# Self-attention softmax sums: four matrix products per key tile, or GpSimd additions and one product per head group

## The chip, the cores and the metric

The kernel is one program on one core of a Trainium2 chip. The metric is device microseconds (us) of that core for the whole program, the median of several executions. Five engines matter here: PE (TensorE, the matrix products), PEld (its weight loads), DVE (VectorE), ACT (ScalarE), POOL (GpSimd); SP (SyncE) issues most of the DMAs.

## The reference, cut to what matters

The program is a gated memory attention, then a decoder block: causal self-attention with 16 heads of 32, a cross-attention, and a feed-forward layer. The change is in the causal self-attention, for a batch of 4 and 512 tokens:

```python
scores = jnp.einsum('bhqd,bhkd->bhqk', q * scale, k)
scores = jnp.where(mask, scores, jnp.finfo(jnp.float32).min)   # causal
p = jax.nn.softmax(scores.astype(jnp.float32), axis=-1).astype(q.dtype)
ctx = jnp.einsum('bhqk,bhkd->bhqd', p, v)
```

The kernel keeps the exponentials unnormalised, computes `exp @ v` and the sums of the exponentials over the keys, and multiplies the rows by the inverse of the sums at the end. It is the way to these sums that the change touches.

## The kernel before

`self_attention()` handles 16 groups (`NG`) of four heads each. Keys are cut into `ST` = 4 tiles of 128; because of the causal mask, key tile `kt` needs only the queries from `kt * 128` on, so its width is 512, 384, 256 and 128 queries a head. Scores are laid out with keys on partitions and queries along the row.

A group has 11 steps (`NU`), one for each of its `score_units`: four of key tile 0 (one head each, 512 wide), four of tile 1 (384 wide), two of tile 2 (two heads of 256), one of tile 3 (four heads of 128). In step `v` PE issues, in an order written out by hand:

- `scores(v + 2)`: mask and score products (L1015, L1018) into one of three PSUM banks;
- one unit of side work for a later group, `fill` (L990, L993: scores with queries on partitions, from which DVE takes row maxima, L961; or L998, a "turn", which turns the maxima of a group so that DVE, L965, and two DMAs of SP can put them as an extra row beside the queries);
- `values(v - 1)`, which does something only behind the last unit of a key tile (steps 4, 8, 10 and step 0 of the next group): four products with the values (L1036) and four with a matrix of ones (L1040), the latter being the sums. The four products of a set write four bands of 32 PSUM partitions, one for each head;
- a second `fill` in one step of each group.

ACT turns each unit of scores into exponentials in the tile `pT_s` (L937), a ring of 3 key tiles. After three units of the next group it copies both PSUM banks, values and sums, to `osb_s` in one instruction (`keep_sums`, L928). DVE then takes the inverses of the sums in four pieces of 128 queries (the "flip" items, L952), one at the head of each of its steps 4 to 7, between the row maxima (L961) that PE's fills feed. DVE does its items strictly in the order of `self_side_work`. POOL waits for the four pieces, multiplies values by inverses (`scale_rows`, L911) and issues the DMA of the result (L914). SP loads queries, keys and values in rings of 4 groups. The side work runs 8 units ahead of its own group, so groups 14 and 15 have little or none of it. Behind the last group DVE alone takes one inverse of 512 (L969) and multiplies (L972).

## Time and profile before

| what | value |
|---|---|
| time, median of 3 runs | 2597.75 us (2596.82 to 2597.81) |
| the profiled execution: its own time | 2612.24 us |
| the profiled execution: span of the trace | 2610.4 us |
| mean granted TensorE clock | 0.886 |
| busy over the span | PE 82%, PEld 53%, DVE 61%, ACT 38%, POOL 18% |
| exponentials L937 | x176, 96.0 us |
| scaling on POOL L911 | x15, 19.1 us |

The span is what the trace covers, from the first to the last instruction; the run's own time is 1.8 us more. Busy time of PE is modelled from pipelined instructions, so a full PE row does not mean that it is at its peak. Start times in the trace are microseconds from the start of the span. Self-attention lies between about 817 and 1052 us.

### The profile page before, as it was taken

Reading aid. Unit: us, or ns where it says so; the run is one execution under the profiler, and the core shown is the slowest. Engines: PE = TensorE matmul, PEld = TensorE weight load, DVE = VectorE, ACT = ScalarE, POOL = GpSimd, SP = SyncE. Lnnn points to the kernel's source line nnn. Section 1 sums busy time; section 2 is a strip of 40 time slices with the busy share of each in tenths; the row PEclk is TensorE's granted clock in tenths of the full one; section 3 lists DMA queues with packets and bytes.
Section 4 is the critical chain, followed back from the end, with each engine's and each line's share of the span. In section 5 each row is a group of like instructions: output and inputs, shape, how many; then the busy total and the mean of one; then the engine's idle time right before and its main releaser. Section 6 shows DMA issues by size and latency. Waiting matters only on the chain. (4 is left out here: it accounts for less than half of the span.)

```text
span 2610.4 us, 33805 instructions
## 1 busy us (share of the span) xinstructions
PE 2129.8 (82%) x12621; PEld 1385.1 (53%) x12638; DVE 1594.5 (61%) x2296; ACT 979.1 (38%) x1723; POOL 469.2 (18%) x474
## 2 busy tenths in 40 slices
PE   5985985985985999447346389999999879999968
PEld 3663664664673555345235234444443457787856
DVE  5186186286284776525325589999998157657544
ACT  1132132132131555123123058888888522222101
POOL 0221221121120111201202002222222312222111
PEclk8987987987986999768777579999999989999979
DMA  4025025025037663474563924444442033333332
GB/s 149 29 78 202 29 81 199 29 87 194 25 95 188 160 163 79 138 158 88 182 157 96 171 39 85 83 80 82 86 87 59 16 115 89 108 105 97 90 95 70
DMA packets 219855, 271.57 MB, mean 104 GB/s; under 512 B 53886, under 2 KB 136450, under 8 KB 217882
## 3 DMA queue, kind: packets, MB, share of 16 engines
q1 hardware_dynamic: 211548, 258.12, 38.8%
q0 software_dynamic: 7856, 10.90, 1.6%
q8 instruction: 116, 1.90, 0.3%
q14 instruction: 47, 0.39, 0.0%
q10 hardware_dynamic: 288, 0.27, 0.0%
HBM read 202.64 MB, written 64.47 MB: 102 GB/s over the span
## 5 line engine op out<-in xcount | busy, mean ns | idle before, releaser
L1521 DVE TENSOR_REDUCE quarters<-ps 128x2 f32<-128x804 f32 x512 | 483.1, 992 | 51.7 <-PE ps L1555 50.0
L1486 ACT ACTIVATE pT_x<-ps 128x512 f32<-128x512 f32 (+1 forms) x832 | 451.5, 595 | 104.0 <-PE ps L1583 76.5
L190 DVE TENSOR_TENSOR w_lo<-w_raw,w_hi 128x512 fp32r<-128x512 f32 (+2 forms) x357 | 278.0, 779 | 12.2
L188 DVE CAST w_hi<-w_raw 128x512 fp32r<-128x512 f32 (+2 forms) x357 | 176.2, 494 | 171.0 <-PE ps L196 93.8
L1555 PE MATMUL ps<-kx_ring,qx_ring 63*128 63x402 f32 x1024 | 234.2, 470 | 47.2 <-DMA kx_ring<-cross_k_by_part 35.4
L1598 PE MATMUL ps<-pT_x,vx_ring 128*17 128x256 f32 (+1 forms) x3328 | 261.4, 387 | 0.2 <-ACT osb_x L1468 0.2
L1555 PEld LDWEIGHTS ps<-kx_ring,qx_ring 63*128 63x128 f32 x1024 | 100.3, 193 | 239.8 <-DVE quarters L1521 124.1
L194 PE MATMUL ps<-mi_h,w_hi 128*128 128x512 f32 (+1 forms) x440 | 175.3, 398 | 34.8 <-issue 24.1
L1583 PE MATMUL ps<-qx_ring,kx_ring 64*128 64x512 f32 (+1 forms) x832 | 175.0, 417 | 6.2 <-ACT pT_x L1486 2.6
L196 PE MATMUL ps<-mi_l,w_hi 128*128 128x512 f32 (+1 forms) x440 | 174.0, 396 | 0.0
L195 PE MATMUL ps<-mi_h,w_lo 128*128 128x512 f32 (+1 forms) x440 | 173.8, 395 | 0.0
L1739 POOL TENSOR_TENSOR sg<-sg,keep_all 128x512 f32<-128x512 f32 (+1 forms) x55 | 87.6, 1592 | 413.3 <-ACT sg L1718 413.3
L961 DVE TENSOR_REDUCE row_max_s<-ps 128x1 f32<-128x384 f32 (+3 forms) x176 | 109.4, 633 | 75.5 <-PE ps L993 74.7
L194 PE MATMUL ps<-att_h,w_hi 128*128 128x512 f32 (+1 forms) x128 | 46.3, 361 | 121.4 <-POOL att_l L1099 121.4
L937 ACT ACTIVATE pT_s<-ps 128x512 f32<-128x512 f32 (+1 forms) x176 | 96.0, 558 | 128.7 <-PE ps L1018 126.6
L1598 PEld LDWEIGHTS ps<-pT_x,vx_ring 128*17 128x17 f32 (+1 forms) x3328 | 55.6, 95 | 111.0 <-issue 70.6
L194 PEld LDWEIGHTS ps<-mi_h,w_hi 128*128 128x128 f32 (+1 forms) x440 | 83.0, 189 | 55.4 <-issue 36.3
L993 PE MATMUL ps<-k_ring,q_ring 96*128 96x128 f32 (+3 forms) x256 | 90.5, 414 | 24.9 <-DMA k_ring<-self_k_by_part 24.9
L1111 DVE TENSOR_TENSOR own<-att_in,keep_expert 128x512 f32<-128x512 f32 x32 | 52.2, 1632 | 93.5 <-DMA att_in<-self_rows_by_batch 93.5
L194 PE MATMUL ps<-xh,w_hi 128*128 128x512 f32 x96 | 44.3, 461 | 76.9 <-DVE xl L304 76.9
L1718 ACT ACTIVATE sg<-ps 128x512 f32<-128x512 f32 (+1 forms) x55 | 32.8, 596 | 191.4 <-PE ps L196 191.4
L332 DVE RECIPROCAL rq<-ps 128x4 f32<-128x4 f32 x4 | 0.7, 184 | 166.9 <-PE ps L415 166.9
(262 smaller groups left out, 4480.1 us busy)
## 6 DMA issues: line engine op xcount, KB each, us to landing
kx_ring<-cross_k_by_part SPq DMA_DIRECT2D x96, 200.2 KB, 7.4
w_raw<-L_xattn_l_qkv SPq DMA_DIRECT2D x48, 256.0 KB, 3.1
w_raw<-L_xattn_v_qkv SPq DMA_DIRECT2D x48, 256.0 KB, 2.7
q_ring<-self_q_by_part SPq DMA_DIRECT2D x48, 256.0 KB, 4.2
k_ring<-self_k_by_part SPq DMA_DIRECT2D x48, 256.0 KB, 6.7
w_raw<-L_xattn_l_gate SPq DMA_DIRECT2D x40, 256.0 KB, 2.9
w_raw<-L_xattn_l_up SPq DMA_DIRECT2D x40, 256.0 KB, 2.9
w_raw<-L_xattn_l_down SPq DMA_DIRECT2D x40, 256.0 KB, 2.7
```

The source lines that it names most:

```text
L188: nc.vector.tensor_copy(hi, raw).then_inc(s_high, 1)
L190: nc.vector.tensor_tensor(out=lo, in0=raw, in1=hi.bitcast(f32), op=ALU.subtract).then_inc(s_split, 1)
L194: nc.tensor.matmul(dst, ah, bh, start=start, stop=False, **how)
L195: nc.tensor.matmul(dst, al, bh, start=False, stop=False, **how)
L196: return nc.tensor.matmul(dst, ah, bl, start=False, stop=stop, **how)
L937: nc.scalar.activation(pT[:, u % 3, j:j + n, 0:width], heads_of(ps[:, SCORES + v % 3, :], n, width), ACT.Exp, scale=SCALE).then_inc(s["s_e ...
L961: nc.vector.tensor_reduce(out=row_max[:, g % 2, j:j + heads, q], in_=heads_of(bank, heads, (q + 1) * P), axis=AX.X, op=ALU.max)\
L1486: nc.scalar.activation(pT[0:kn, u % 3, j, :], ps[0:kn, 5 + v % 3, :], ACT.Exp, scale=SCALE)\
L1521: nc.vector.tensor_reduce(out=quarters[:, g % 2, pair, :, q, quarter], in_=ps[:, at:at + 2, 0:MAXW], axis=AX.X, op=ALU.max)\
L1555: last = nc.tensor.matmul(ps[:, at + par, 0:MAXW], q_r[rows, g % RING, pair, q * P:(q + 1) * P], k_r[rows, g % RING, pair, k0:k0 + MAXW], ...
L1583: nc.tensor.matmul(ps[0:kn, 5 + (v + par) % 3, :], k_r[rows, g % RING, pair, k0:k0 + kn], q_r[rows, g % RING, pair, :], start=True, stop=T ...
L1598: last = nc.tensor.matmul(ps[j * HD:j * HD + CHD + 1, 4, queries], v_r[0:kn, g % RING, kt, j, :], pT[0:kn, u % 3, j, queries], start=kt == ...
```

## The change

POOL adds up the exponentials of a group's four key tiles into a new tile `acc_s`, and PE multiplies that one by the matrix of ones, once for a group (`total`), in step 3 of the next group. The tile `pT_s` keeps only tiles 1 to 3; tile 0's exponentials are written by ACT straight into `acc_s` (`exponentials`), a ring of 3 groups. POOL's order in a group is now: add tile 1 (`add_up(g, 1)`), scale the rows of the group before, add tile 2, add tile 3. ACT's copy is split in two, the values after three units of the next group (`keep_rows`), the sums after six (`keep_sums`), with a semaphore each. The four flips move from DVE's steps 4 to 7 to steps 6 to 9.

```diff
--- before.py
+++ after.py
@@ -814,7 +814,7 @@
             start, feed, given, by_step = feed[:first], feed[first:], 0, []
             for v in range(groups * steps):
                 g, i = divmod(v, steps)
-                now = [("flip", g - 1, i - 4)] if g and 4 <= i < 8 else []
+                now = [("flip", g - 1, i - 6)] if g and 6 <= i < 10 else []
                 due = -(-(v + 1) * (maxima + 1) // steps)
                 while feed and given < due:
                     now.append(feed.pop(0))
@@ -826,7 +826,7 @@
         def self_attention():
 
             RING, KQ_LOADS = 4, 6
-            names = ("s_kq0 s_kq1 s_kq2 s_kq3 s_v0 s_v1 s_v2 s_v3 s_one s_fill s_used s_so s_sh s_sc s_exp s_pv s_ob "
+            names = ("s_kq0 s_kq1 s_kq2 s_kq3 s_v0 s_v1 s_v2 s_v3 s_one s_fill s_used s_so s_sh s_sc s_exp s_pv s_acc s_sum s_ob s_os "
                      "s_rq s_at s_up0 s_up1 s_last s_end")
             ctx, sems = stage(names)
             s = dict(zip(names.split(), sems))
@@ -847,9 +847,15 @@
                 v_r = sb("v_ring", [P, RING, ST, P], ctx=ctx)
                 row_max = sb("row_max_s", [P, 2, 4, ST], ctx=ctx)
                 shift = sb("shift_s", [4 * ST, 2, P], f32r, ctx=ctx)
-                pT = sb("pT_s", [P, 3, 4, S], ctx=ctx)
+                pT, acc = sb("pT_s", [P, 3, 4, S - P], ctx=ctx), sb("acc_s", [P, 3, 4, S], ctx=ctx)
                 osb, att = sb("osb_s", [P, 2, 2, S], ctx=ctx), sb("att_s", [P, 2, S], ctx=ctx)
                 rq_rows = sb("rq_rows_s", [P, S], ctx=ctx)
+
+                def exponentials(u, j, n, width):
+
+                    g, kt = divmod(u, ST)
+                    later = g * (ST - 1) + kt - 1
+                    return pT[:, later % 3, j:j + n, 0:width] if kt else acc[:, g % 3, j:j + n, 0:width]
 
                 def heads_of(bank, n, width):
 
@@ -913,31 +919,60 @@
                             pool.wait_ge(s["s_at"], g + 1)
                             pool.dma_start(att_d[g // GB, :, g % GB, :], att[:, g % 2, :]).then_inc(s[f"s_up{g % 2}"], 16)
 
-                        for g in range(NG - 1):
-                            scale_rows(g)
+                        def add_up(g, kt):
+
+                            v = max(i for i in ends if ends[i] == kt)
+                            pool.wait_ge(s["s_exp"], NU * g + v + 1)
+                            if kt == 1:
+                                pool.wait_ge(s["s_pv"], ST * g + 1)
+                            else:
+                                pool.wait_ge(s["s_acc"], (ST - 1) * g + kt - 1)
+                            rest = acc[:, g % 3, :, kt * P:S]
+                            nc.gpsimd.tensor_tensor(out=rest, in0=rest, in1=exponentials(ST * g + kt, 0, 4, S - kt * P), op=ALU.add)\
+                                .then_inc(s["s_acc"], 1)
+
+                        for g in range(NG):
+                            add_up(g, 1)
+                            if g:
+                                scale_rows(g - 1)
+                            add_up(g, 2)
+                            add_up(g, 3)
                         for i in range(2):
                             pool.wait_ge(s[f"s_up{i}"], 16 * (NG // 2 - i))
 
                     @block.scalar
                     def _(act):
-                        def keep_sums(g):
+                        def keep_rows(g):
 
                             act.wait_ge(s["s_pv"], ST * (g + 1))
                             if g >= 2:
                                 act.wait_ge(s["s_at"], g - 1)
-                            nc.scalar.activation(osb[:, g % 2, :, :], ps[:, VALUES:SUMS + 1, :], ACT.Copy).then_inc(s["s_ob"], 1)
+                            nc.scalar.activation(osb[:, g % 2, 0, :], ps[:, VALUES, :], ACT.Copy).then_inc(s["s_ob"], 1)
+
+                        def keep_sums(g):
+
+                            act.wait_ge(s["s_sum"], g + 1)
+                            if g >= 2:
+                                act.wait_ge(s["s_at"], g - 1)
+                            nc.scalar.activation(osb[:, g % 2, 1, :], ps[:, SUMS, :], ACT.Copy).then_inc(s["s_os"], 1)
 
                         for v in range(NG * NU):
                             g, i = divmod(v, NU)
                             kt, j, n = score_units[i]
                             u, width = g * ST + kt, S - kt * P
                             act.wait_ge(s["s_sc"], v + 1)
-                            if u >= 3 and j == 0:
-                                act.wait_ge(s["s_pv"], u - 2)
-                            nc.scalar.activation(pT[:, u % 3, j:j + n, 0:width], heads_of(ps[:, SCORES + v % 3, :], n, width),
+                            if j == 0 and kt == 0 and g >= 3:
+                                act.wait_ge(s["s_sum"], g - 2)
+                            if j == 0 and kt and g:
+                                act.wait_ge(s["s_pv"], u - 3)
+                                act.wait_ge(s["s_acc"], (ST - 1) * g + kt - ST + 1)
+                            nc.scalar.activation(exponentials(u, j, n, width), heads_of(ps[:, SCORES + v % 3, :], n, width),
                                                  ACT.Exp, scale=SCALE).then_inc(s["s_exp"], 1)
                             if g and i == 2:
+                                keep_rows(g - 1)
+                            if g and i == 5:
                                 keep_sums(g - 1)
+                        keep_rows(NG - 1)
                         keep_sums(NG - 1)
 
                     @block.vector
@@ -946,7 +981,7 @@
                             g = o[1]
                             if o[0] == "flip":
                                 cut = slice(o[2] * P, (o[2] + 1) * P)
-                                dve.wait_ge(s["s_ob"], g + 1)
+                                dve.wait_ge(s["s_os"], g + 1)
                                 if g:
                                     dve.wait_ge(s["s_at"], g)
                                 nc.vector.reciprocal(rq_rows[:, cut], osb[:, g % 2, 1, cut]).then_inc(s["s_rq"], 1)
@@ -965,6 +1000,7 @@
                                     nc.vector.tensor_copy(shift[:, g % 2, :], bank[0:4 * ST, 0:P]).then_inc(s["s_used"], 1)
                         g = NG - 1
                         dve.wait_ge(s["s_ob"], NG)
+                        dve.wait_ge(s["s_os"], NG)
                         dve.wait_ge(s["s_at"], g)
                         nc.vector.reciprocal(rq_rows[:, :], osb[:, g % 2, 1, :]).then_inc(s["s_last"], 1)
                         dve.wait_ge(s["s_last"], 1)
@@ -1033,13 +1069,20 @@
                                 if g:
                                     pe.wait_ge(s["s_ob"], g)
                             for m in range(4):
-                                nc.tensor.matmul(ps[m * HD:(m + 1) * HD, VALUES, kt * P:S],
-                                                 v_r[:, g % RING, kt, m * HD:(m + 1) * HD], pT[:, u % 3, m, 0:width],
-                                                 start=kt == 0, stop=kt == ST - 1)
+                                last = nc.tensor.matmul(ps[m * HD:(m + 1) * HD, VALUES, kt * P:S],
+                                                        v_r[:, g % RING, kt, m * HD:(m + 1) * HD], exponentials(u, m, 1, width)[:, 0, :],
+                                                        start=kt == 0, stop=kt == ST - 1)
+                            last.then_inc(s["s_pv"], 1)
+
+                        def total(g):
+
+                            pe.wait_ge(s["s_acc"], (ST - 1) * (g + 1))
+                            if g:
+                                pe.wait_ge(s["s_os"], g)
                             for m in range(4):
-                                last = nc.tensor.matmul(ps[m * HD:(m + 1) * HD, SUMS, kt * P:S], ones[:, 0:HD],
-                                                        pT[:, u % 3, m, 0:width], start=kt == 0, stop=kt == ST - 1)
-                            last.then_inc(s["s_pv"], 1)
+                                last = nc.tensor.matmul(ps[m * HD:(m + 1) * HD, SUMS, :], ones[:, 0:HD], acc[:, g % 3, m, :],
+                                                        start=True, stop=True)
+                            last.then_inc(s["s_sum"], 1)
 
                         for o in start:
                             fill(o)
@@ -1051,11 +1094,14 @@
                                 scores(v + 2)
                             if todo:
                                 fill(todo.pop(0))
+                            if v % NU == 3 and v > NU:
+                                total(v // NU - 1)
                             if v:
                                 values(v - 1)
                             for o in todo:
                                 fill(o)
                         values(NG * NU - 1)
+                        total(NG - 1)
                 clear(sems)
 
         def add_projection(b, tiles, early_v):
```

## Rows read from the trace of the kernel before

**Rows 1.** Windows: busy PE, PEld, DVE, ACT, POOL; granted clock; DMA share; GB/s.

```profile
845.00:1047.00 202.00, 200.84 (x1809) 115.62 (x1824) 145.38 (x226) 105.94 (x184) 27.94 (x30) 1.00 0.56 133
1047.00:1052.00 5.00, 0.07 (x4) 0.00 (x0) 3.77 (x2) 1.02 (x1) 0.00 (x0) 1.00 0.00 2
1052.00:1053.00 1.00, 0.00 (x0) 0.00 (x0) 0.27 (x1) 0.00 (x0) 0.00 (x0) 0.55 0.00 0
...
869.77:883.18 13.41, 13.41 (x123) 7.81 (x125) 10.20 (x17) 6.98 (x12) 1.85 (x2) 1.00 0.67 171
```

**Rows 2.** Waits from 853 to 1028: engine line waited for, total us, times, longest.

```profile
POOL att_s L911 <- DVE rq_rows_s L952: 200.5, 13, 65.6
ACT pT_s L937 <- PE ps L1018: 78.2, 92, 1.9
```

**Rows 3.** Timeline of PE, one group: start us, us, instruction.

```profile
928.44 0.85 PE L1036 MATMUL ps<-pT_s,v_ring 128*32 128x384 f32 x8
...
929.11 0.83 PE L1040 MATMUL ps<-pT_s,ones 128*32 128x384 f32 x8
...
931.34 0.64 PE L1036 MATMUL ps<-pT_s,v_ring 128*32 128x256 f32 x8
...
931.80 0.61 PE L1040 MATMUL ps<-pT_s,ones 128*32 128x256 f32 x8
...
933.15 0.43 PE L1036 MATMUL ps<-pT_s,v_ring 128*32 128x128 f32 x8
...
933.40 0.40 PE L1040 MATMUL ps<-pT_s,ones 128*32 128x128 f32 x8
...
936.40 0.23 PE L1015 MATMUL ps<-mask_kq,ident_b 128*128 128x128 bf16 x1
...
936.81 0.63 PE L1036 MATMUL ps<-pT_s,v_ring 128*32 128x512 f32 x3
...
937.69 1.21 PE L1040 MATMUL ps<-pT_s,ones 128*32 128x512 f32 x8
...
938.84 0.23 PE L1015 MATMUL ps<-mask_kq,ident_b 128*128 128x128 bf16 x1
```

**Rows 4.** Timeline of POOL, ACT and DVE in the same group.

```profile
929.18 1.27 POOL L911 TENSOR_TENSOR att_s<-osb_s,rq_rows_s 128x512 f32<-128x512 f32 x1 [11.25 <-DVE rq_rows_s L952]
...
930.75 0.58 POOL L914 DMA_DIRECT2D self_rows_by_batch<-att_s  x1 [0.30 <-POOL att_s L911]
...
939.33 0.49 ACT L937 ACTIVATE pT_s<-ps 128x384 f32<-128x384 f32 x1 [1.94 <-PE ps L1018]
...
939.70 0.69 DVE L961 TENSOR_REDUCE row_max_s<-ps 128x2 f32<-128x512 f32 x1 [0.56 <-PE ps L993]
...
940.31 0.94 DVE L952 RECIPROCAL rq_rows_s<-osb_s 128x128 f32<-128x128 f32 x1
...
941.17 0.49 DVE L961 TENSOR_REDUCE row_max_s<-ps 128x1 f32<-128x384 f32 x1
...
941.58 0.94 DVE L952 RECIPROCAL rq_rows_s<-osb_s 128x128 f32<-128x128 f32 x1
```

**Rows 5.** Groups of POOL instructions, whole span: xcount, busy us, mean ns, idle before.

```profile
L1739 POOL TENSOR_TENSOR sg<-sg,keep_all 128x512 f32<-128x512 f32 x50 | 79.9, 1597 | 379.4 <-ACT sg L1718 379.4
L291 POOL TENSOR_TENSOR acc<-acc,pT 128x512 f32<-128x512 f32 x44 | 57.1, 1298 | 80.4 <-ACT pT L280 80.2
...
L1945 POOL MEMSET const-bfloat16-1.0<- 128x1 bf16 x1 | 0.1, 101 | 0.0
```

**Rows 6.** Timeline: `scores(6)` of groups 1, 14 and 15, and the last inverse.

```profile
855.94 0.23 PE L1015 MATMUL ps<-mask_kq,ident_b 128*128 128x128 bf16 x1
...
1030.32 0.23 PE L1015 MATMUL ps<-mask_kq,ident_b 128*128 128x128 bf16 x1
...
1040.27 0.23 PE L1015 MATMUL ps<-mask_kq,ident_b 128*128 128x128 bf16 x1 [0.58 <-ACT pT_s L937]
...
1048.19 3.35 DVE L969 RECIPROCAL rq_rows_s<-osb_s 128x512 f32<-128x512 f32 x1 [5.04 <-ACT osb_s L928]
```

## Prediction

> **What bounds the kernel now.** I read the page first (PE is the busiest engine of the span, POOL the idlest), then the stage by windows, then its waits, then PE's timeline for one group. In the windows, PE is busy for 200.84 of 202 us and the clock is granted in full (1.00, 2.4 GHz); one group takes 13.41 us, PE busy in all of it, DVE 10.20, ACT 6.98, POOL 1.85 [rows 1]. In the waits, ACT waits for PE's scores (78.2 us) and POOL nearly all the time for DVE's inverses (200.5 us) [rows 2]; in this steady part PE's own list has no wait of weight on any engine. So PE sets the period, and whatever leaves PE shortens it, until another loop becomes longer. Which loops there are is the question, because the change makes PE wait, in the middle of its fixed order, for the end of a chain through ACT, DVE and POOL.
>
> **What PE saves.** From the first value product of a key tile to the first product of sums there pass 0.88 us (936.81 to 937.69), 0.67, 0.46 and 0.25 us for tiles 0 to 3 [rows 3]. The second set costs as much again, so taking it out saves 2.26 us a group. One set of 512 comes back: from 937.69 to the next full-array product at 938.84 it is 1.15 us [rows 3], about 0.1 of it the change of shape. Net saving about 1.1 us, or 1.0 with one more change of shape on the way in (my choice): PE alone would need 12.4 us a group.
>
> **What POOL's additions cost.** They have 1536, 1024 and 512 elements a partition. The nearest row is the same operation in the memory attention, 1.30 us for 512 (1.27 for the product L911) [rows 4, 5]. No larger one is in the trace. Scaled in full, 1024 take 2.54 and 1536 take 3.82 us; if the 0.10 us of a one-element memset is a fixed part [rows 5], 2.44 and 3.61. I take 2.49, 3.7 and 1.27; the two ways of scaling are close. The upper bound is 1.60 us for 512, what POOL's products take in the feed-forward stage, 3.12 ns an element [rows 5]. Below the scaled values I see no reason to go.
>
> The Trainium skill (GPSIMD Engine Reference, Performance versus the Vector engine) gives 4497 ns for an addition of 2048 elements on this engine. With the 1.27 us for 512 of the trace, an estimate from that page is 2.10 ns for each further element, so 2.35 and 3.42 us; the loop below would be 0.14 us shorter. No row here shows an addition of that size.
>
> **The loop that closes.** In PE's order, `total(g)` stands in step 3 of group g + 1. Behind it in PE's queue are `scores(6)`, the turn, `values` of tile 0, `scores(7)` and all later steps. It waits for `add_up(g, 3)`, which is behind `add_up(g, 2)`, which is behind `scale_rows(g - 1)`, and that waits for the four inverses of group g - 1. These need DVE's steps 6 to 9 of group g, and DVE's step 6 needs the row maxima of PE's step 5, which comes behind `total(g - 1)`. So from `total(g - 1)` a chain runs back to `total(g)`, and the group can't be shorter than it. Counted from the start T of a `total`:
>
> 1. `total` itself, 1.15 us to `scores(6)` [rows 3].
> 2. `scores(6)` to the reduction of step 5: 936.40 to 939.70 is 3.30 us; the removed set of tile 0 takes 0.88 off, 2.42 us [rows 3, 4]. At T + 3.57. The copy of the sums (at T + 1.1, some 0.6 us) is done well before.
> 3. DVE: that reduction to the next item 0.61 us, an inverse 0.86 us, a reduction of 384 0.41 us (start to start) [rows 4]. The order is reduction, flip, reduction, flip, reduction, flip, reduction, flip: 0.61 + 3 x 0.41 + 3 x 0.86 + 0.94 (the last in full) = 5.36 us. At T + 8.93.
> 4. To the start of `scale_rows` 0.09 us; its product 1.27, 0.30 to its DMA, whose issue takes 0.58 (929.18 to 931.33) [rows 4]. At T + 11.2. All of that is in front of the second addition in POOL's order.
> 5. Additions: 2.49 us, then 0.30 for the wait of one POOL instruction on the last (as between L911 and L914), then 1.27 [rows 4, 5]; 0.1 to PE. At T + 15.3.
>
> The first addition is not in the sum: exponential 7 ends at 939.82, 0.12 us behind the start of the reduction [rows 4], so it runs from T + 3.7 to T + 7.4, under DVE's inverses, with 1.5 us to spare. If DVE were done sooner, this addition would be the longer branch (rival 2).
>
> So the group takes 15.3 us instead of 13.41, and PE, with 12.4 us of work, stands for some 2.9 us in front of `total`. **The flips' move** by two steps is therefore not free: on DVE it costs nothing (10.2 of 13.4 us busy [rows 1]), but the last inverse lands two steps later, and these two steps are on the chain. DVE's row maxima run up to a microsecond behind PE after the flips; PE's waits for them fall into the 2.9 us.
>
> **What costs nothing.** ACT's two copies for one: a second fixed cost on an engine busy 6.98 of 13.41 us [rows 1]. Its new waits (on `s_acc` and `s_sum`, for the freed ring places) look at additions of one group and a product of two groups before. SP's order is unchanged; its loads wait on the same counts of scores and values, three or more groups back. `keep_rows` comes where the old copy was.
>
> **The stage.** Up to `total(0)` there is no chain: group 0's scaling does not exist yet, and its additions end about when PE arrives. `scores(6)` of group 1 stood at 855.94 [rows 6]; with one group's sums gone, `total(0)` starts 2.3 us before that. Then:
> - 13 groups, `total(0)` to `total(13)`: 13 x (15.3 - 13.41) = +24.6 us. (855.94 + 13 x 13.41 = 1030.27, the row has 1030.32 [rows 6].)
> - Group 14 to 15: nothing is left to fill, so DVE is free and its flips end at about T + 5.3. The chain is POOL's own: exponential 7 at T + 3.5, additions and scaling 0.05 + 3.7 + 2.15 + 2.49 + 0.30 + 1.27 + 0.1, T + 13.5. Before, 9.95 us (1030.32 to 1040.27 [rows 6]): +3.5 us.
> - Tail: again 13.5 us to the last `total`, whose matmuls take 1.1, then the copy of 512, 0.6, and hops: the last inverse starts at T + 15.3. Before, 1040.27 to 1048.19, 7.9 us [rows 6]: +7.4 us. Nothing covers this; everything behind the stage moves with it.
>
> Sum: -2.3 + 24.6 + 3.5 + 7.4 = +33 us. The profiled execution would go from 2612.24 to about 2645 us; it lies 14.5 us above the median of the runs shown, and I carry the difference over to that median: 2597.75 + 33 = 2631 us, 1.3% slower.
>
> **Rivals.**
> 1. *PE stays the bound; faster.* If the additions took less than about a quarter of what I take (1.1 us for both and the hop, where I have 4.06), the loop would be under PE's 12.4 us. Then -2.3 - 13 x 1.0 - 1 - 1.5 = -18 us, 2580 us. For it: POOL is idle for 11.5 of 13.4 us [rows 1], and its 7.5 us of additions fit in that by busy time. Against: only the latency counts, and 1.30 us for 512 is measured 44 times [rows 5]. 5%.
> 2. *POOL alone sets the loop.* If the inverses land earlier than I read from DVE's order, scaling starts behind the first addition, at T + 7.4, and the loop is 13.7 us: -2.3 + 3.7 + 3.5 + 7.4 = +12 us, 2610 us. Against: each flip stands in DVE's order behind a reduction that PE feeds. 7%.
> 3. *POOL is slowed beside DVE.* At 1.60 us for 512, scaling and two additions cost 1.4 us more in the loop, and the last two loops 2.5 us more each: 33 + 18 + 5, 2654 us. Against: L911 takes 1.27 us in this very stage with DVE at work, and DVE has mostly PSUM inputs and one-input inverses there [rows 4]. 8%. The Trainium skill (GPSIMD Engine Reference, Specifications) says that GpSimd shares its SBUF interfaces with VectorE and is held up by instructions with two SBUF inputs or in a two-port mode; by that rule the one-input inverses and maxima would not hold POOL up. No row here shows what slows L1739.
> 4. *The clock falls in the new gaps.* PE would stand for 2.9 us in every group. If that dropped it to 1.2 GHz for the chain's PE part, another 2.6 us a group, 14 x 2.6 = 36 us, 2667 us. Against: behind the stage PE is idle from 1047 on, and the granted clock is 1.00 until 1052 [rows 1], a gap of 5 us. 4%.
>
> **How the numbers follow.** My forecast has 76%. Its own range: hops and waits of 0.3 to 0.5 us less in each of 13 loops make -6, some slower additions or waits of PE on DVE on the chain +13: 2624 to 2644. Rivals 3 and 4 and part of 1 lie outside the range that I give, 2610 to 2650, which takes in rival 2. A measurement of this kernel can tell about 0.2% (5.2 us) from no change. Faster: rival 1 and a little for a misread loop, 6%; same, 4%; slower, 90%.
>
> **What would show it.** In the profile after: PE waits for POOL once a group, 2.5 to 3 us, in front of the product of `acc_s`; PE's busy share of the stage falls to some 80%, clock still 1.00; POOL waits for DVE's inverses once a group, 1.5 us, and goes from `scale_rows` to the third addition without a gap of weight; the period is 15.3 us; additions take 3.7, 2.5 and 1.27 us; from the last score product to the last inverse it is some 11 us instead of 4. The prediction is wrong if PE shows no wait for POOL (rival 1), if POOL never waits for DVE (rival 2), or if the additions take over 3 us for 1024 elements (rival 3).

## The result, and the profile after

The changed kernel takes 2643.89 us (median of 5 runs, 2641.39 to 2650.51) against 2597.75 us: a ratio of 1.0179, 95% interval 1.0165 to 1.0193. It is 46 us slower. Forecast were 2631 us, 2610 to 2650.

The page after, its engine part (engine, busy us, share of the span, instructions):

```profile
PE 2122.8 (80%) x12254; PEld 1367.7 (52%) x12254; DVE 1590.8 (60%) x2296; ACT 984.1 (37%) x1739; POOL 583.5 (22%) x522
```

PE's busy time is only 7 us lower than before. The removed products ran four abreast, 0.88 us a set for the widest [rows 3], and what PE does at half clock is busy for longer: in the stage alone its busy time is 229.8 us, against 225.9 before. POOL has 114 us more, and still has 22% of the span. By busy shares nothing explains 46 us. The waits from 853 to 1050 us do (engine line waited for: total, times, longest), to be read against [rows 2]:

```profile
POOL acc_s L931 <- ACT pT_s L969: 64.1, 13, 6.4
...
PE ps L1083 <- POOL acc_s L931: 29.5, 12, 2.6
...
POOL att_s L917 <- DVE rq_rows_s L987: 22.1, 12, 2.1
```

The two lines with twelve waits are the new loop: PE's product of sums (L1083) waits for POOL's last addition up to 2.6 us in each group, and POOL's scaling (L917) waits for DVE's inverses. A window of the stage (length; busy PE, PEld, DVE, ACT, POOL; granted clock; DMA share; GB/s), against [rows 1]:

```profile
853.00:1050.00 197.00, 167.50 (x1184) 87.56 (x1176) 118.63 (x195) 89.00 (x160) 108.30 (x61) 0.91 0.51 122
```

PE is busy for 85% of it instead of 99%, and the granted clock is 0.91 in the mean instead of 1.00. Shorter windows around two of PE's gaps, the same columns:

```profile
929.00:931.60 2.60, 0.22 (x2) 0.01 (x1) 0.95 (x2) 0.38 (x1) 2.46 (x2) 1.00 1.07 267
931.60:933.00 1.40, 1.32 (x10) 0.36 (x10) 0.00 (x0) 0.18 (x1) 0.03 (x1) 1.00 0.21 76
933.00:934.00 1.00, 1.00 (x10) 0.39 (x10) 0.28 (x1) 0.80 (x2) 0.00 (x0) 0.65 0.02 8
934.00:936.00 2.00, 2.00 (x9) 0.68 (x5) 0.00 (x0) 0.12 (x1) 0.00 (x0) 0.50 0.02 4
...
937.00:939.00 2.00, 2.00 (x19) 1.55 (x21) 2.00 (x4) 1.54 (x3) 2.00 (x1) 1.00 0.00 0
944.00:948.00 4.00, 1.70 (x17) 1.28 (x16) 2.14 (x4) 1.34 (x3) 3.76 (x3) 0.87 1.06 243
948.00:949.00 1.00, 1.00 (x8) 0.18 (x8) 0.00 (x0) 0.00 (x0) 0.00 (x0) 0.50 0.23 82
949.00:953.00 4.00, 4.00 (x22) 1.13 (x14) 0.28 (x1) 1.09 (x2) 0.00 (x0) 0.50 0.03 6
...
954.00:956.00 2.00, 2.00 (x18) 1.69 (x16) 1.94 (x4) 1.19 (x2) 1.94 (x1) 1.00 0.00 0
```

They show where the clock goes: after a gap of 2.5 us (929 to 931.6) the clock is 1.00 for a moment, then 0.50 (1.2 GHz) from 933 to 936; in the next turn it is already down within 944 to 948 and stays so to 953.

One turn of the loop in POOL's timeline (start us, us, instruction), against [rows 4]:

```profile
888.92 3.48 POOL L931 TENSOR_TENSOR acc_s<-acc_s,pT_s 128x1536 f32<-128x1536 f32 x1 [4.95 <-ACT pT_s L969]
894.45 1.28 POOL L917 TENSOR_TENSOR att_s<-osb_s,rq_rows_s 128x512 f32<-128x512 f32 x1 [2.05 <-DVE rq_rows_s L987]
896.02 0.58 POOL L920 DMA_DIRECT2D self_rows_by_batch<-att_s  x1 [0.30 <-POOL att_s L917]
896.62 3.77 POOL L931 TENSOR_TENSOR acc_s<-acc_s,pT_s 128x1024 f32<-128x1024 f32 x2
904.08 3.47 POOL L931 TENSOR_TENSOR acc_s<-acc_s,pT_s 128x1536 f32<-128x1536 f32 x1 [3.69 <-ACT pT_s L969]
```

And DVE's timeline in a later turn:

```profile
920.26 0.69 DVE L996 TENSOR_REDUCE row_max_s<-ps 128x2 f32<-128x512 f32 x1 [2.31 <-PE ps L1029]
920.87 0.94 DVE L987 RECIPROCAL rq_rows_s<-osb_s 128x128 f32<-128x128 f32 x1
921.73 0.49 DVE L996 TENSOR_REDUCE row_max_s<-ps 128x1 f32<-128x384 f32 x1
922.14 0.93 DVE L987 RECIPROCAL rq_rows_s<-osb_s 128x128 f32<-128x128 f32 x1
...
924.26 0.49 DVE L996 TENSOR_REDUCE row_max_s<-ps 128x1 f32<-128x384 f32 x1
924.67 0.93 DVE L987 RECIPROCAL rq_rows_s<-osb_s 128x128 f32<-128x128 f32 x1
```

DVE's order is the one that the prediction wrote down: reduction, inverse, four times over, 5.34 us from the start of the first to the end of the last (920.26 to 925.60). POOL then runs through scaling, the DMA's issue and two additions without a gap. From one first addition to the next it is 15.16 us here (888.92 to 904.08), and 16 to 17.6 us in most other groups.

The end of the stage, all engines' timeline, against [rows 6]:

```profile
1060.85 1.93 PE L1083 MATMUL ps<-acc_s,ones 128*32 128x512 f32 x8 [2.36 <-POOL acc_s L931]
...
1075.96 1.93 PE L1083 MATMUL ps<-acc_s,ones 128*32 128x512 f32 x8 [4.37 <-POOL acc_s L931]
...
1090.67 1.93 PE L1083 MATMUL ps<-acc_s,ones 128*32 128x512 f32 x8 [7.17 <-POOL acc_s L931]
...
1093.36 3.35 DVE L1005 RECIPROCAL rq_rows_s<-osb_s 128x512 f32<-128x512 f32 x1 [11.38 <-ACT osb_s L957]
```

The time of a whole run moves by several microseconds from run to run, and the kernel before had medians of 2597.23, 2604.36 and 2606.84 us beside the three sets of experiments. So the experiments are also compared by the length of the stage in their traces: from the first side product (L993 before, L1029 after) to the start of the last inverse of 512. Before it is 817.55 to 1048.19, 230.6 us; with the change 814.71 to 1093.36, 278.7 us: +48.0 us. The profiled execution before was the odd one outside of this stage, 14.5 us over its median. What a profile's span holds beside the stage lies between 2363 and 2380 us over all twelve profiles (these two and the ten of the experiments), so one execution's whole time says little about a few microseconds.

### The profile page after: what moved, and what is told of

Its sections match the earlier page's. It is cut to its first block and busy times, and to the rows that moved or that the text cites. A ratio compares the mean times of both kernels' runs of the same rounds, so it can differ in the third digit from the quotient of the medians.

```text
span 2642.1 us, 33192 instructions
## 1 busy us (share of the span) xinstructions
PE 2122.8 (80%) x12254; PEld 1367.7 (52%) x12254; DVE 1590.8 (60%) x2296; ACT 984.1 (37%) x1739; POOL 583.5 (22%) x522
## 5 line engine op out<-in xcount | busy, mean ns | idle before, releaser
L996 DVE TENSOR_REDUCE row_max_s<-ps 128x1 f32<-128x384 f32 (+3 forms) x176 | 104.1, 620 | 63.0 <-PE ps L1029 62.5
L931 POOL TENSOR_TENSOR acc_s<-acc_s,pT_s 128x1536 f32<-128x1536 f32 (+2 forms) x48 | 113.5, 2365 | 126.5 <-ACT pT_s L969 123.7
L1145 POOL TENSOR_TENSOR att_l<-own,att_h 128x512 fp32r<-128x512 f32 x32 | 46.7, 1459 | 267.1 <-ACT att_h L1138 267.1
L1768 ACT ACTIVATE hid_h<-prod 128x512 fp32r<-128x512 f32 (+1 forms) x55 | 34.8, 634 | 177.0 <-DVE prod L1849 177.0
```

The lines of the kernel that those rows point to most:

```text
L931: nc.gpsimd.tensor_tensor(out=rest, in0=rest, in1=exponentials(ST * g + kt, 0, 4, S - kt * P), op=ALU.add)\
L996: nc.vector.tensor_reduce(out=row_max[:, g % 2, j:j + heads, q], in_=heads_of(bank, heads, (q + 1) * P), axis=AX.X, op=ALU.max)\
```

## The experiments

Each is the changed kernel with the edit shown, unless it says otherwise. "T" is the start of a product of sums, as in the prediction.

**1. The inverses back in DVE's steps 4 to 7** (the order of the other engines stays).

```diff
-                now = [("flip", g - 1, i - 6)] if g and 6 <= i < 10 else []
+                now = [("flip", g - 1, i - 4)] if g and 4 <= i < 8 else []
```

> The changed kernel with the inverses back in DVE's steps 4 to 7. Theory (the loop from one product of sums to the next runs through the last inverse): the inverses land at T + 6.6, the first addition's end at T + 7.2 becomes the longer branch, the loop is 7.2 + 2.15 + 3.8 = 13.2 us, PE's gap before the product shrinks to under 1 us and the clock stays at 1.00; about 2604 us. Rival (the additions themselves, or their traffic, cost the time, and the place of the inverses doesn't matter): the period stays at 16 us and the time at 2644 us.

Measured: 2605.04 us, ratio to the kernel before 1.0036 (1.0017 to 1.0055), stage 239.6 us. Two first additions and what is between them in POOL's timeline:

```profile
897.58 3.47 POOL L931 TENSOR_TENSOR acc_s<-acc_s,pT_s 128x1536 f32<-128x1536 f32 x1 [3.69 <-ACT pT_s L969]
900.99 1.31 POOL L917 TENSOR_TENSOR att_s<-osb_s,rq_rows_s 128x512 f32<-128x512 f32 x1
902.59 0.58 POOL L920 DMA_DIRECT2D self_rows_by_batch<-att_s  x1 [0.30 <-POOL att_s L917]
...
910.69 3.47 POOL L931 TENSOR_TENSOR acc_s<-acc_s,pT_s 128x1536 f32<-128x1536 f32 x1 [3.68 <-ACT pT_s L969]
```

The period is 13.1 us, POOL no longer waits for DVE (scaling has no idle time before it), and PE's longest wait for POOL is 0.7 us. One constant gives back 39 of 48 us, and the granted clock is 1.00 from 853 to 1030 us. The work is the same, so with the additions there it is the place of the inverses in the loop that costs. The kernel is still 0.4% slower than the one before.

**2. POOL's scaling behind the third addition.**

```diff
                             add_up(g, 1)
-                            if g:
-                                scale_rows(g - 1)
                             add_up(g, 2)
                             add_up(g, 3)
+                            if g:
+                                scale_rows(g - 1)
```

> The changed kernel with POOL's scaling of the group before behind the third addition instead of behind the first; all additions stay. Theory (latency of one loop): the additions end at T + 11.0, before PE arrives at T + 12.4, PE waits for nothing, the period is 12.4 us, the tail is about 5 us longer than before the change; 2588 us, range 2583 to 2595, faster than the kernel before. Rival (POOL's work itself slows the other engines): over 2600 us, since not one addition is gone.

Measured: 2595.01 us, ratio 0.9996 (0.9982 to 1.0009), stage 225.3 us. POOL's timeline:

```profile
879.47 7.41 POOL L931 TENSOR_TENSOR acc_s<-acc_s,pT_s 128x1536 f32<-128x1536 f32 x3 [2.78 <-ACT pT_s L969]
886.84 1.27 POOL L917 TENSOR_TENSOR att_s<-osb_s,rq_rows_s 128x512 f32<-128x512 f32 x1
888.40 0.58 POOL L920 DMA_DIRECT2D self_rows_by_batch<-att_s  x1 [0.30 <-POOL att_s L917]
891.88 3.46 POOL L931 TENSOR_TENSOR acc_s<-acc_s,pT_s 128x1536 f32<-128x1536 f32 x1 [2.90 <-ACT pT_s L969]
```

The end of the stage, all engines:

```profile
1023.44 1.63 PE L1083 MATMUL ps<-acc_s,ones 128*32 128x512 f32 x8 [2.67 <-POOL acc_s L931]
...
1035.85 1.94 PE L1083 MATMUL ps<-acc_s,ones 128*32 128x512 f32 x8 [5.19 <-POOL acc_s L931]
...
1038.54 3.35 DVE L1005 RECIPROCAL rq_rows_s<-osb_s 128x512 f32<-128x512 f32 x1 [9.41 <-ACT osb_s L957]
```

All additions are there, 7.4 us in a row, and from 853 to 1010 us PE waits for POOL nowhere: 12.3 to 12.9 us a group. In the steady part the additions hold nobody up once their chain doesn't run through the scaling, and the rival falls. The stage is 5.3 us shorter than before the change; of the whole time that is 0.2%, about the lower end of the interval. The expectation was 2588 us and faster than the kernel before; the measured time is at the upper end of its range and level with the kernel before. In the tail 5.2 us of PE's idle time stand in front of the last product of sums.

**3. Ten products of constants in PE's gap.** They write the bank that the product of sums then overwrites, so the output is unchanged.

```diff
                         def total(g):

-                            pe.wait_ge(s["s_acc"], (ST - 1) * (g + 1))
                             if g:
                                 pe.wait_ge(s["s_os"], g)
+                                for _ in range(10):
+                                    nc.tensor.matmul(heads_of(ps[:, SUMS, :], 4, P), ident_b[:, :], mask_qk[:, :, :],
+                                                     start=True, stop=True, skip_group_check=True)
+                            pe.wait_ge(s["s_acc"], (ST - 1) * (g + 1))
```

> The changed kernel with ten products of constants (512 columns, bf16, into the bank of the sums, which the real product overwrites) put before the wait for POOL in each group but the first: 2.1 us of PE work in a gap of 2.5 us. Theory (1.0 to 1.2 us a group is the granted clock, which falls in the gap): every loop takes 14.9 to 15.1 us at clock 1.00, 14 us less in all, about 2630 us although PE does more. Rival (the loops of 16 to 17.6 us have another cause, such as hops between engines): no change, 2644 us, or slower by what the products overrun.

Measured: 2632.29 us, ratio 1.0135 (1.0116 to 1.0154), stage 261.7 us, 17 us less than with the change as it is (the medians differ by 11.6 us, where 14 were expected). A window of the stage (columns as above):

```profile
850.00:1040.00 190.00, 186.35 (x1340) 98.36 (x1364) 126.19 (x207) 93.28 (x169) 112.42 (x62) 1.00 0.55 129
```

One gap in PE's timeline:

```profile
938.06 2.33 PE L1082 MATMUL ps<-mask_qk,ident_b 128*128 128x512 bf16 x10
940.69 1.07 PE L1086 MATMUL ps<-acc_s,ones 128*32 128x512 f32 x8 [0.30 <-POOL acc_s L931]
```

The clock is 1.00 throughout this window, every loop but the first (15.0) takes 14.86 us, and PE still waits 0.30 us for POOL, so the chain is untouched. The changed kernel as it is has the same number: from product of sums to product of sums, three of its 13 loops take 14.86 us and the first 15.0, all four at full clock, and the nine in which the clock falls take 16.3 to 17.5. More work made the kernel faster, by what the clock had taken.

**4. The kernel before, with the inverses alone moved to steps 6 to 9** (the first experiment's line the other way round).

> The kernel before the change with one edit of it alone, the inverses in DVE's steps 6 to 9. Theory (they matter only through POOL's chain, which doesn't exist here): no difference, 2596 to 2600 us. Rival (DVE's row maxima come late behind them and hold PE up): up to 1 us in each of 14 groups, 2605 to 2612 us.

Measured: 2596.95 us, ratio 0.9995 (0.9985 to 1.0005), stage 230.7 us. The same place of the inverses that costs 39 us with the additions costs nothing without them.

**5. The product of sums two steps later, its copy behind the eighth exponential unit.**

```diff
-                            if v % NU == 3 and v > NU:
+                            if v % NU == 5 and v > NU:
                                 total(v // NU - 1)
...
-                            if g and i == 5:
+                            if g and i == 7:
                                 keep_sums(g - 1)
```

> The changed kernel with the product of sums in PE's step 5 instead of 3 and ACT's copy of the sums behind the eighth exponential unit instead of the sixth; POOL's order and the inverses stay. Theory (what counts is the chain through the last inverse): exponential 7 and the first addition now lie in front of the product, the inverses can start at T + 1.9, the last lands at T + 6.6, scaling and two additions bring the loop to 12.7 us instead of 16.1, PE stands for less than 1 us; the stage, from its first side product to the last inverse, takes about 235 us (230.7 before the change, 278.7 with it), 2600 us in all. Rival (a loop can't be shortened by a later product, the wait only moves): over 2635 us.

Measured: 2607.08 us, ratio 1.0012 (1.0000 to 1.0023), stage 229.5 us against the 235 expected. The whole time is level with the kernel before or 0.2% above it. The loop is 12.62 us (12.7 expected), clock 1.00; POOL's timeline:

```profile
910.52 1.27 POOL L917 TENSOR_TENSOR att_s<-osb_s,rq_rows_s 128x512 f32<-128x512 f32 x1 [3.11 <-DVE rq_rows_s L987]
912.09 0.58 POOL L920 DMA_DIRECT2D self_rows_by_batch<-att_s  x1 [0.30 <-POOL att_s L917]
912.69 7.32 POOL L931 TENSOR_TENSOR acc_s<-acc_s,pT_s 128x1024 f32<-128x1024 f32 x3
923.14 1.27 POOL L917 TENSOR_TENSOR att_s<-osb_s,rq_rows_s 128x512 f32<-128x512 f32 x1 [3.12 <-DVE rq_rows_s L987]
```

POOL still waits 3.1 us for the inverses, but DVE can start on them sooner: the chain from product to product now has the copy, the inverses, the scaling and two additions, and nothing of PE's steps 4 and 5. The next group's first addition follows in the same row of three ("x3") and is off the chain. The rival (the wait only moves) falls: PE waits 0.2 us for POOL in each group.

**6. Both: later product and scaling last.**

> The edit before and POOL's scaling behind the third addition together. Theory: with scaling last the steady part already has PE's own period of 12.4 us, so only the gap of 2.7 us in the last full groups can shrink: stage 223 us against 225.3, 2592 us. Rival (some wait is left in the steady part of the version with scaling last): over 5 us better than that one.

Measured: 2595.62 us, ratio 0.9973 (0.9960 to 0.9986), stage 221.3 us, 4.0 less than in experiment 2 and 1.7 less than expected. The rival (a wait left in the steady part) doesn't hold: the period is the same 12.35 us, and the gain lies at both ends, in group 1 (12.7 us from the first to the second first addition, 13.9 in experiment 2) and in the last two groups.

**7. Scaling last, and no additions in the last two groups**, where PE has no side work. There PE makes four products of sums a key tile, as before the change. Left out of the cut below are POOL, which makes no additions in these two groups, and ACT's waits, which follow.

```diff
+                            if g >= NG - 2:
+                                if kt == 0:
+                                    pe.wait_ge(s["s_os"], g)
+                                for m in range(4):
+                                    last = nc.tensor.matmul(ps[m * HD:(m + 1) * HD, SUMS, kt * P:S], ones[:, 0:HD],
+                                                            exponentials(u, m, 1, width)[:, 0, :],
+                                                            start=kt == 0, stop=kt == ST - 1)
                             last.then_inc(s["s_pv"], 1)
...
-                            if v % NU == 3 and v > NU:
+                            if v % NU == 3 and v > NU and v // NU - 1 < NG - 2:
                                 total(v // NU - 1)
...
-                        total(NG - 1)
```

> Scaling last, and in the last two groups, where PE has no side work left, the sums as before the change: four products a key tile by PE and no additions. Theory (the steady part gains 1.0 us in each of 13 groups, the last two groups and the tail lose some 8 us by POOL's latency): these 8 us come back, stage about 217 us against 230.7 before the change, 2584 us, 0.5% faster than the kernel before. Rival (the tail is bound by the copy and the inverse of 512, not by the additions): stage 225 us, no gain on the version with scaling last.

Measured: 2595.05 us, ratio 0.9960 (0.9946 to 0.9975), stage 224.3 us: 7 more than expected, and close to the rival's 225. But the tail did what it should, against the rival: the last inverse of 512 starts 6.8 us behind the first inverse of group 14 (1030.59 to 1037.41), where experiment 2 has 12.8 (1025.74 to 1038.54). The loss is at the start, in windows with the columns as above:

```profile
840.00:845.00 5.00, 3.67 (x30) 2.34 (x28) 2.34 (x4) 2.29 (x4) 3.99 (x2) 1.00 0.59 129
845.00:850.00 5.00, 4.72 (x28) 2.06 (x28) 1.55 (x3) 1.79 (x3) 3.09 (x2) 0.62 1.05 231
850.00:855.00 5.00, 5.00 (x26) 3.41 (x18) 2.47 (x4) 1.99 (x4) 0.00 (x0) 0.50 0.58 127
855.00:860.00 5.00, 5.00 (x23) 1.13 (x23) 0.97 (x2) 1.27 (x3) 0.00 (x0) 0.51 0.01 3
860.00:865.00 5.00, 5.00 (x39) 3.34 (x38) 4.17 (x7) 2.89 (x6) 3.82 (x2) 1.00 0.25 64
```

In this execution the clock went down at about 846 us, behind a wait of PE for SyncE's shift DMA at 845.28 (1.6 us), and stayed at 0.50 until 860. In experiment 2's profile the same wait, 1.53 us, was followed by 1.00 all along. From group 0's first addition to group 1's it took 20.2 us here and 13.9 there, 6.2 us more.

**8. Experiment 7 with the later product** (step 5, in group 14 step 3; the copy to match).

```diff
-                            if v % NU == 3 and v > NU and v // NU - 1 < NG - 2:
+                            if v % NU == (5 if v // NU < NG - 2 else 3) and v > NU and v // NU - 1 < NG - 2:
                                 total(v // NU - 1)
...
-                            if g and i == 5:
+                            if g and i == (7 if g < NG - 2 else 5):
                                 keep_sums(g - 1)
```

> The version with the sums of the last two groups by PE, plus the product of sums in step 5 (step 3 only in group 14). Theory: that version's profile lost 6 us because the granted clock fell at 845 us, behind a wait for a DMA at the stage's start, and stayed down for 15 us; without that its stage is 218 us, and the later product gives 1 us in group 1: stage 217 us (230.7 before the change), 2585 us, 0.5% faster than the kernel before. Rival (the edit itself cost these 6 us): stage 224 us or more in every execution, no faster than the version with scaling last.

Measured: 2591.99 us against 2606.84 us of the kernel before on the same chip, ratio 0.9949 (0.9929 to 0.9969). It is faster than both kernels, by 0.5% against the one before. The end of its stage, in DVE's timeline:

```profile
1034.70 3.35 DVE L1009 RECIPROCAL rq_rows_s<-osb_s 128x512 f32<-128x512 f32 x1 [3.43 <-ACT osb_s L961]
```

Stage 218.3 us (816.41 to 1034.70), 12.4 less than before the change, at a granted clock of 1.00 from 850 to 1010. The rival (experiment 7's own edit costs the 6 us) falls by this one profile, in which that edit is still there; the 6 us of experiment 7 were the clock at the stage's start.

**9. The kernel before, profiled again.**

> The kernel before, profiled a second time. Its first profiled execution was 14.5 us above its median. Theory: the self-attention stage takes the same 230.7 us, and the 14 us lie outside of it, in stages that both kernels share. Rival: the stage itself varies by as much, and the comparison of the stages is worth little.

Measured: span 2598.4 us, 12.0 less than in the first profile, stage 230.7 us (811.86 to 1042.61). The first profile's excess is outside of the stage.

**10. The changed kernel, profiled again.**

> The changed kernel, profiled a second time. Theory (the chain sets a loop of 15.1 us at full clock, and how often the clock falls in the gap varies): full-clock loops take 15.0 to 15.2 us again, the others 16 to 17.6, in another order, and the stage takes 276 to 282 us. Rival (the long loops come from certain groups, such as DMAs of a new batch): the same groups are long in both profiles.

Measured: stage 282.1 us (817.56 to 1099.69), the upper end of the expected range; this execution took 2660.48 us, 16.6 over the median, and 13 of these lie outside of the stage. From group 0's first addition to group 1's it took 20.1 us instead of 13.8, as in experiment 7: the granted clock is 0.66 in the mean from 845 to 865 us, and 1.00 in the first profile of the same kernel. The loops, from first addition to first addition, are 16.4, 15.1, 16.4, 16.2, 15.1, 16.4, 16.1, 15.2, 16.4, 16.0, 17.6, 15.1, 16.2 us; in the first profile 16.6, 16.1, 15.2, 16.4, 16.0, 17.6, 15.1, 16.4, 16.2, 15.1, 16.4, 16.1, 17.2. The long one of 17.6 us is group 6's in the first and group 11's in the second, and the short ones have changed places too, so it isn't a matter of certain groups or their DMAs.

The stages side by side:

| kernel | stage, us | ratio to before (95%) |
|---|---|---|
| before | 230.6, 230.7 | 1 |
| before, inverses moved | 230.7 | 0.9995 (0.9985 to 1.0005) |
| changed | 278.7, 282.1 | 1.0179 (1.0165 to 1.0193) |
| changed, products in the gap | 261.7 | 1.0135 (1.0116 to 1.0154) |
| changed, inverses early | 239.6 | 1.0036 (1.0017 to 1.0055) |
| changed, product later | 229.5 | 1.0012 (1.0000 to 1.0023) |
| changed, scaling last | 225.3 | 0.9996 (0.9982 to 1.0009) |
| scaling last, product later | 221.3 | 0.9973 (0.9960 to 0.9986) |
| scaling last, last groups by PE | 224.3 | 0.9960 (0.9946 to 0.9975) |
| all three | 218.3 | 0.9949 (0.9929 to 0.9969) |

## Why the prediction was right, and where its sum was short

**The loop: right.** PE waits for POOL once a group, POOL for DVE once a group, in the places named. Experiments 1, 2 and 5 each cut the chain at another link (the inverses' place, the scaling in front of the additions, the product's place in PE's order), and each brought 39 to 53 us of the stage back with no addition removed; 17 of these can be the clock's share (experiment 3), the rest is the chain's. Experiment 4 shows that the inverses' move matters only with the chain there. Of the signs that the prediction named, most came: PE's wait in front of the product of sums is 2.45 us (2.5 to 3 forecast), POOL's wait for the inverses 1.75 to 2.1 us (1.5), and from the end of the last score product to the last inverse it is 11.3 us (11). One failed: the clock does not stay at 1.00, and the period is 16.02 us, not 15.3.

**The sum, term by term**, in the stage: forecast +33.2, measured +48.0.

| term | forecast | measured |
|---|---|---|
| up to `total(0)` | -2.3 | -0.5 (852.60 - 814.71 against 855.94 - 817.55) |
| 13 groups | +24.6 | +33.9 (852.60 to 1060.85 is 16.02 a group, against 13.41) |
| group 14 to 15 | +3.5 | +5.2 (1060.85 to 1075.96, 15.1, against 9.95) |
| tail | +7.4 | +9.5 (1075.96 to 1093.36, 17.4, against 7.92) |

**The mis-sized term is the loop, by the clock.** The prediction took 15.3 us for a group with the clock at 1.00 throughout, and held a falling clock for a rival of 4%, because the 5 us of idle PE behind the stage had passed at 1.00 [rows 1]. That was half a reading: the next line of the same rows has 0.55, so the clock fell right at the end of these 5 us, where PE had nothing to do and nothing was lost. In the new loop the fall comes late as well, some 4 us after PE stopped (929.2 to 933.3), when the gap of 2.5 us is over and PE is at work again. Experiment 3 splits the term: at full clock the loop is 14.86 us, 0.44 shorter than forecast (-5.7 us over 13), and the clock adds 16.02 - 14.86 = 1.16 us a group (+15.1 us). With the clock up in these 13 groups, experiment 3's stage is 31.1 us longer than before the change, where the prediction summed up 33.2. The last two groups lose by it too: the granted clock is 0.72 in the mean from 1058 to 1093 us, their products of sums take 1.93 us, in the groups at full clock 1.07, and POOL's first addition starts 5.7 and 5.3 us behind the product of sums, where the sum had 3.5:

```profile
1066.55 3.47 POOL L931 TENSOR_TENSOR acc_s<-acc_s,pT_s 128x1536 f32<-128x1536 f32 x1 [5.75 <-ACT pT_s L969]
...
1081.30 3.45 POOL L931 TENSOR_TENSOR acc_s<-acc_s,pT_s 128x1536 f32<-128x1536 f32 x1 [5.40 <-ACT pT_s L969]
```

Rival 4 was thus no alternative but a part of the likeliest case. Its price of 2.6 us is what one loop lost (17.5 us, the clock down from 947 to 953.8); eight others lost some 1.5 us, and four nothing, although in three of these PE had waited for 2.45 us as in the others. Why the clock falls in one loop and not in the next is not shown. That the time came out inside of the stated range is so in part by luck: the loop at full clock was a little shorter than forecast, and the clock, which was left out of the sum, took less than rival 4 had set for it.

**Why the loop at full clock is shorter.** Both additions take 3.77 us together, where the sum had 4.06: a little under half of the difference is the addition of 1024, the rest that the third addition starts 0.14 us behind the second and not the 0.30 us that I carried over from a DMA's issue. The remaining 0.15 us of 0.44 are not taken apart. The sizes were close: 3.47, 2.37 and 1.26 us for 1536, 1024 and 512 elements, against 3.7, 2.49 and 1.27. The Trainium skill (GPSIMD Engine Reference, Performance versus the Vector engine), from whose figure the prediction had the estimates of 3.42 and 2.35 us, agrees with the trace better than my scaling did.

**The start.** One group's saving of 2.3 us became 0.5: at 846.64 PE waited 1.3 us for SyncE's DMA of group 1's shifts, for which only a weight load waited before, 0.7 us (849.43). The prediction passed over that DMA as unchanged, but PE now comes to it sooner.

```profile
846.64 0.23 PE L1051 MATMUL ps<-mask_kq,ident_b 128*128 128x128 bf16 x1 [1.34 <-DMA q_ring<-shift_by_head]
```

**The other rivals.** POOL beside DVE wasn't slowed: scaling takes 1.28 us (1.27 before), and the pair of additions 3.77 us in the loop and 3.75 at 1086.87, where DVE is idle. POOL behind its first addition as the bound (rival 2) is what experiment 1 makes: 13.1 us a group, where the prediction gave 13.7. PE as the bound (rival 1) needs no cheaper additions, only another order: experiment 2's 12.3 us a group, against 12.4 worked out.

## What to carry to other kernels

When work moves from the busiest engine to an idle one, compare latencies round the loop, not busy shares: write down what the new wait stands in front of, follow its producers back until you come to the same instruction one turn earlier, and add up that circle. If it is longer than the period, try the order on the engines in it first (here one moved call, 53 us of stage), and look at the tail by itself, where nothing covers the chain: here the old way was better there by 3 us of stage (experiment 6 to experiment 8).

A gap that a change opens on TensorE in every period can cost more than its length, as it did here; price the clock into the likeliest case, and read a row of the clock on past the end of the gap.

## What the runs showed of the hardware

- The granted clock of TensorE fell to 1.2 GHz behind gaps of 2.3 to 2.6 us that came once a group, in nine of 13 loops, in eight of them when PE was back at work already. Behind the stage of the kernel before, it fell some 5 us after PE had stopped [rows 1]. It cost 1.16 us a group in the mean, and ten products of constants in the gap took the loss away (experiment 3). With waits of 0.6 to 0.75 us for POOL once a group (experiment 1) it stayed at 1.00. The Trainium skill (TensorE: Matmul & The Clock Gate, A second HAM failure mode) describes a clock that swings between its two levels when PE idles briefly and often between groups of products; this trace agrees.
- The same short wait at the stage's start (1.3 to 1.6 us, for a DMA) was followed by full clock in one execution and by 14 us at 1.2 GHz in another, in the two profiles of the changed kernel itself (experiment 10) and in experiments 2 and 7, which are alike up to there: some 6 us from the first addition to the next that no edit made.
- POOL's addition of fp32 takes 2.15 ns for each further element (1261, 2366, 3467 ns for 512, 1024, 1536), with 0.16 us left over as a fixed part; one that depends on the one before starts 0.14 us behind its end.
